# A reordering on TensorE in the heavy attention stage: select, scatter, turn two units, then project the queries

## The chip, the core and the metric

The kernel runs on one NeuronCore of a Trainium2 chip. The metric is the device time of one execution in microseconds (us), the median of several runs. The core's engines are named as in the profile: PE (TensorE, matrix products; its weight loads are the rows of PEld), DVE (VectorE), ACT (ScalarE), POOL (GpSimd) and SP (SyncE, which issues DMAs). Each engine runs its own instructions in program order; they wait for each other through semaphores.

## The reference

Four transformer layers over 16 sequences of 256 tokens with 128 channels (float32), each an attention and a feed-forward part with a residual and a layer norm. The change lies in the feed-forward part of the third layer (`L2_ffn`), in its heavy branch. The setup draws this part's `x` for another batch, but what runs is the 16 x 256 tokens of the stream.

```python
def route(x, routing_token, num_tokens):            # queries: 128 tokens, keys/values: 256
    s = einsum('bnd,d->bn', x, routing_token)
    scores = coor_descent(s, min(num_tokens * 9/8, n))
    sel_scores, sel_idx = top_k(scores, num_tokens)
...
light_out = light_local_attn(x, ...)                 # windows of 128 tokens
routed_q  = take_along_axis(x, idx_q[..., None], 1)  # the 128 chosen tokens of each sequence
routed_out = heavy_attn(routed_q, routed_kv, scores_kv, ...)   # 8 heads of 64, 128 queries x 256 keys
heavy_out = zeros_like(x).at[arange(b)[:, None], idx_q].set(routed_out * scores_q)
return light_out + heavy_out
```

## The kernel before

`l2_ffn` runs a routing start, a light attention stage (tiles named `a5l_...`), a routing finish and the heavy attention stage (`a5h_...`). Both attention stages, and that of layer four, come from one function, `wide_stage`. The heavy one lasts from about 1872 to 2118 us of the profiled execution.

`wide_stage` works in **slots**. A heavy slot handles one sequence (one of 16): four "units" of 128 queries x 512 score columns (two heads each). `all_quads` writes slots 0 to 3 out (`i == 0`), then runs a hardware loop of three rounds with four slots each (slots 4 to 15), then five tail slots in which only older work is finished. I number the slots 0 to 15 in order of time. In slot *s*, PE does, in the order written in the function `slot` under `block.tensor`:

- `scores` (L2554): q times k of sequence *s* into banks 0 to 3. It waits until the projections of this sequence have been copied out (`step_out0`, `step_out1`) and the older contents of the banks are done.
- `values` (L2586): probabilities times v of sequence *s-2*.
- `scatter` (L3138, from slot 3 on): puts the 128 results of sequence *s-3* back to their tokens by a product with its one-hot matrix, into bank 3. It waits for DVE's last score copy of the slot (`masked`, unit 3), which frees bank 3.
- group 0 of the projection steps, for sequence *s+1*: step "g" (L3041 and L3043) turns the one-hot matrix and picks the chosen tokens, into bank 0; ACT copies the result to `picked` (L3058); step "q" (L3050) multiplies `picked` by the query weights, into bank 1, and so waits for that copy; ACT copies it to `q` (L3060).
- `turn` of units 0 and 1 of sequence *s-1* (L2567): transposes of the probabilities into banks 4 and 5.
- group 1, the two key steps (L2983), then `project` (L2601) for sequence *s-2*, then group 2, the two value steps (L2980), then `turn` of units 2 and 3.

`picked` is a ring of four tiles, so the tile that g of slot *s* fills is the one that the scatter of slot *s* reads: ACT's copy L3058 waits for `scattered` (line `act.wait_ge(S["scattered"], ...)` in `SelectedSteps.act`).

ACT has a fixed order too: copy of the values (L2827), `picked`, `q`, the exponentials of units 0 and 1 (L2813, whose scores DVE has copied at L2667), the copy of turned unit 0 (L2820), the two key copies (L2991), the exponentials of unit 2, the copy of `project`'s result (L3132), the exponentials of unit 3 and the copy of turned unit 2. DVE copies scores, adds the scattered rows into X (L3146), copies turned units 1 and 3 (L2675), builds the one-hot matrix (L3032) and copies the values of group 2 (L3007). POOL normalizes (L2907) and copies x for later sequences.

Of the kernel before, what the change touches and what calls it, by code (L numbers as in the profile page):

```python
# [323 lines left out]
def total(i, each, k):  # L324

    return max(i * each + k, 0) if isinstance(i, int) else i * each + k
# [2046 lines left out]
NQ = 128  # L2373
# [41 lines left out]
def wide_stage(core, ctx, n, hd, steps, epilogue, moments=True, next_weights=(), ghost=None, weights_of=None, beside=None):  # L2415
# [3 lines left out]
    NQ, NE = len(hd.quads), len(hd.ends)  # L2419
# [14 lines left out]
    with mem:  # L2434
# [31 lines left out]
        groups = []  # L2466
# [20 lines left out]
        def in_loop(i):  # L2487
            return not (isinstance(i, int) and i == ROUNDS)

        def lagging(i, s, lag):  # L2490

            q = s - lag
            if (q >= 0 and in_loop(i)) or (q < 0 and not (isinstance(i, int) and i == 0)):
                return [q]
            return []

        def ending(i, s, lag):

            return [e for e in range(-E, E) if end_of(e) == s - lag and lagging(i, s, lag)]
# [6 lines left out]
        def halves_of(q):  # L2506


            b, k = divmod(q, NQ)
            return [(b * NH + before[k] + m, units, b * NE + e, place)  # L2510
                    for m, (units, e, place) in enumerate(hd.parts[k])]
# [27 lines left out]
        def _(pe):  # L2539
            pe.wait_ge(core.weights_in[wk], loaded_count(wk))  # L2540

            def scores(i, s):
                b, q = divmod(s, NQ)
                pe.wait_ge(S["masked"], total(i, 4 * R, 4 * s) + CREDIT)
                for lane in range(2):
                    pe.wait_ge(S[f"step_out{lane}"], total(i, NB * NS // 2, issued(s, lane)) + CREDIT)
                epilogue.wait_banks(pe, S, lambda lag: total(i, E, begun(s, lag)))
                for p in (0, 2):
                    pair = hd.quads[q][p:p + 2]
                    for m in range(len(pair[0][3])):  # L2550
                        for j, (qt, k0, kw, heads) in enumerate(pair, p):
                            c, odd = divmod(heads[m], 2)
                            r0 = 64 * odd
                            mm = pe.matmul(sbank[j][:, m * kw:(m + 1) * kw],  # L2554
                                           B["q"][b % 2][r0:r0 + 64, c, qt * P:(qt + 1) * P],
                                           B["k"][b % 2][r0:r0 + 64, c, k0:k0 + kw], start=True, stop=True)
                            if m == len(heads) - 1:
                                mm.then_inc(S["scores"], 1)

            def turn(i, q, j):  # L2560
                pe.wait_ge(S["normalized"], total(i, 4 * R, 4 * q + j + 1) + CREDIT)
                if j < 2:
                    pe.wait_ge(S[f"turned_out{j + 2}"], total(i, R, q) + CREDIT)
                else:
                    pe.wait_ge(S[f"turned_out{j - 2}"], total(i, R, q + 1) + CREDIT)
                for c in range(4):
                    mm = pe.transpose(tbank[j % 2][:, c * P:(c + 1) * P], pr[j][:, c * P:(c + 1) * P], ident)  # L2567
                mm.then_inc(S["turned"], 1)

            def values(i, s):  # L2570
                b, q = divmod(s % R, NQ)
                for g, units, e, place in halves_of(s):
                    for j in units:
                        pe.wait_ge(S[f"turned_out{j}"], total(i, R, s + 1) + CREDIT)
                    pe.wait_ge(S["evacuated"], total(i, NB * NH, g - 1) + CREDIT)
                    for p in units[::2]:
                        pair = hd.quads[q][p:p + 2]
                        qt, k0, kw, _ = pair[0]
                        nb = kw // P
                        for m in range(len(pair[0][3])):  # L2580
                            for kb in range(nb):
                                for j, unit in enumerate(pair, p):
                                    h = unit[3][m]
                                    r0, c0 = 64 * (h % 2), h // 2 % 4 * P
                                    col = (m * nb + kb) * P
                                    mm = pe.matmul(obank[g % 2][r0:r0 + 64, c0:c0 + P],  # L2586
                                                   B["v"][b % hd.ring][:, k0 // P + kb, h * 64:(h + 1) * 64],
                                                   pt[j][:, col:col + P], start=(kb == 0), stop=(kb == nb - 1))
                    mm.then_inc(S["values"], 1)
# [4 lines left out]
            def project(i, s, e):  # L2594
                y = epilogue.bank_of(e)
                masks_done(i, s, y)
                epilogue.wait_last(pe, S, lambda k: total(i, E, e + k))
                pe.wait_ge(S["evacuated"], total(i, NB * NH, halves_until(end_of(e)) + max(
                    m + 1 for m, (_, at, _) in enumerate(hd.parts[hd.ends[e % NE]]) if at == e % NE)) + CREDIT)
                for k in range(hd.chunks):  # L2600
                    mm = pe.matmul(sbank[y][:, 0:DM], on[e % 2][:, k * P:(k + 1) * P], epilogue.wo[:, k * DM:(k + 1) * DM],  # L2601
                                   start=(k == 0), stop=(k == hd.chunks - 1))
                mm.then_inc(S["projected"], 1)

            def scatter(i, s, e):
                masks_done(i, s, 3)
                epilogue.scatter(pe, B, S, i, e, sbank[3])

            def step(i, b, j, first=False):

                seq = NB * i + b
                if not first:
                    pe.wait_ge(S[steps.out_of(j)], steps.nth_out(seq, j) - 1 + CREDIT)
                    masks_done(i, b * NQ - NQ + j * NQ // NS, j % 2)
                elif j >= len(FIRST):
                    pe.wait_ge(S[steps.out_of(j)], steps.nth_out(0, j - len(FIRST)) + CREDIT)
                if j == 0:
                    pe.wait_ge(S["x_copied"], seq + 1 + CREDIT)
                steps.pe(pe, core, B, S, FIRST[j % len(FIRST)] if first else sbank[j % 2], j, b, seq).then_inc(S["step_mm"], 1)
# [1 line left out]
            for j in range(NS):  # L2621
                step(0, 0, j, True)

            def steps_in(i, s, group):
                if in_loop(i):
                    for j in groups[s % NQ][group]:
                        step(i, s // NQ + 1, j)

            def slot(i, s):
                if in_loop(i):  # L2630
                    scores(i, s)
                for q in lagging(i, s, LV):
                    values(i, q)
                if epilogue.scatters:
                    for e in ending(i, s, LS):
                        scatter(i, s, e)
                steps_in(i, s, 0)
                for q in lagging(i, s, LT):
                    turn(i, q, 0)
                    turn(i, q, 1)  # L2640
                steps_in(i, s, 1)
                for e in ending(i, s, LP):
                    project(i, s, e)
                steps_in(i, s, 2)
                for q in lagging(i, s, LT):
                    turn(i, q, 2)
                    turn(i, q, 3)

            all_quads(pe, slot)

        @block.vector
# [947 lines left out]
```

## Time and profile before

| what | us |
|---|---|
| median of 3 runs | 2816.76 (2816.34 to 2819.14) |
| the profiled execution | 2823.93 |
| its span | 2822.2 |
| slots 0 to 15 of the heavy stage, first scores to the last turned unit | 1882.1 to 2106.2 |
| a usual heavy slot, scores to scores | 14.0 to 14.4 |
| slot 4, the first of the hardware loop | 19.0 |

Over the whole span PE is busy 83% (with weight loads beside it, 65%), DVE 67%, ACT 49%, POOL 49%. TensorE's granted clock is a mean of 0.942 of full speed. "Busy" of PE includes the drain of pipelined products, so the starts of consecutive groups say more than their durations: what PE takes for a group is the distance from its start to the next group's start where nothing is waited for.

### The profile page before, as it was taken

The page shows a single profiled execution, that of the slowest core. Times are in us where ns is not written, and L with a number is a line of the kernel's source. Part 1 is how long each engine was busy: PE and PEld are TensorE (multiplying, and loading weights), DVE is VectorE, ACT ScalarE, POOL GpSimd, SP SyncE. Part 2 cuts the span into 40 slices and gives each one's busy share as a digit, 9 for nine tenths or more (in the row PEclk, how much of TensorE's full clock was granted, in tenths as well). Part 3 has the DMA queues.
Part 4 walks back from the last instruction along what each step waited for, and adds up shares of the span by engine and source line. Part 5 has one row for each costly group of instructions (what it writes and reads, how often), then busy time and mean ns, then how long its engine had stood idle before and what let it go on. Part 6 is the DMA issues. An engine that isn't in the chain of part 4 may idle for free. (4 is left out here: it accounts for less than half of the span.)

```text
span 2822.2 us, 72090 instructions
## 1 busy us (share of the span) xinstructions
PE 2353.0 (83%) x21404; PEld 1825.2 (65%) x21404; DVE 1897.4 (67%) x8141; ACT 1390.2 (49%) x3317; POOL 1385.6 (49%) x1580
## 2 busy tenths in 40 slices
PE   6888888778689980869999799958987999999986
PEld 5666666545366660857777577747775777777755
DVE  4666666656488872657888589955555777767746
ACT  2333333322366650646666456634554666666624
POOL 4666666400366644547778265623332554554501
PEclk9999999989799995989999899989998999999978
DMA  2000000033100011220000100000000000000001
GB/s 73 2 1 0 0 0 0 20 86 79 53 2 0 0 38 42 65 82 2 0 0 0 39 2 1 0 1 2 0 0 23 2 1 0 0 0 0 0 1 31
DMA packets 38281, 45.51 MB, mean 16 GB/s; under 512 B 6160, under 2 KB 28777, under 8 KB 37804
## 3 DMA queue, kind: packets, MB, share of 16 engines
q1 hardware_dynamic: 35820, 38.89, 4.9%
q0 software_dynamic: 2304, 4.79, 0.5%
q8 instruction: 67, 1.10, 0.2%
q14 instruction: 90, 0.74, 0.1%
HBM read 36.62 MB, written 9.74 MB: 16 GB/s over the span
## 5 line engine op out<-in xcount | busy, mean ns | idle before, releaser
L1102 POOL TENSOR_TENSOR a_sm<-a_sm,a_top 128x512 f32<-128x512 f32 x512 | 524.2, 1041 | 279.9 <-DVE a_top L900 278.0
L1025 ACT ACTIVATE a_pr<-a_sm 128x512 f32<-128x512 f32 x512 | 315.2, 626 | 239.8 <-POOL a_sm L1102 151.6
L900 DVE CUSTOM_DVE_ANT_0 a_sm<-bank,cst 128x256 f32<-128x256 f32 (+1 forms) x1024 | 301.0, 353 | 106.3 <-PE bank L762 104.2
L776 PE MATMUL bank<-cst,a_pr 128*128 128x128 f32 x2304 | 309.5, 276 | 1.3 <-ACT a_pt L1035 0.9
L2907 POOL TENSOR_TENSOR a_pr<-a_sm,a_rden 128x512 f32<-128x512 f32 x192 | 197.4, 1049 | 228.1 <-DVE a_rden L2693 227.7
L776 PEld LDWEIGHTS bank<-cst,a_pr 128*128 128x128 f32 x2304 | 257.0, 141 | 33.5 <-issue 23.6
L908 DVE COPY a_pt<-bank 128x512 f32<-128x512 f32 x272 | 186.7, 686 | 132.5 <-PE bank L776 132.4
L1035 ACT ACTIVATE a_pt<-bank 128x512 f32<-128x512 f32 x304 | 177.3, 589 | 87.9 <-PE bank L776 83.9
L2667 DVE CUSTOM_DVE_ANT_0 a_sm<-bank,cst 128x256 f32<-128x256 f32 (+1 forms) x512 | 149.9, 354 | 52.4 <-PE bank L2554 45.1
L796 PEld LDWEIGHTS bank<-a_pt,a_v 128*32 128x32 f32 x4608 | 119.6, 110 | 99.9 <-issue 89.1
L796 PE MATMUL bank<-a_pt,a_v 128*32 128x128 f32 x4608 | 156.5, 276 | 17.8 <-issue 6.9
L900 DVE CUSTOM_DVE_ANT_0 a_sm<-bank,a_bias 128x256 f32<-128x256 f32 (+1 forms) x512 | 148.4, 353 | 25.3 <-PE bank L762 21.9
L2983 PE MATMUL bank<-a_xs,W 128*128 128x256 f32 x544 | 142.0, 396 | 17.0 <-ACT a_q L2996 10.8
L762 PE MATMUL bank<-a_kx,a_q 32*128 32x512 f32 (+1 forms) x896 | 111.0, 576 | 41.2 <-DVE a_on L918 32.3
L2907 POOL TENSOR_TENSOR a5h_pr<-a5h_sm,a5h_rden 128x512 f32<-128x512 f32 x64 | 65.7, 1047 | 159.6 <-DVE a5h_rden L2693 159.6
L900 DVE DVE_READ_ACCUMULATOR2_ANT a_top<- 128x1 f32 x1536 | 127.9, 83 | 0.0
L2813 ACT ACTIVATE a_sm<-a_sm,a_top 128x256 f32<-128x256 f32 x256 | 127.1, 505 | 0.0
L1092 POOL COPY a_xs<-XT 128x256 f32 (+1 forms) x54 | 21.5, 400 | 209.3 <-SPq L629 209.3
L2983 PEld LDWEIGHTS bank<-a_xs,W 128*128 128x128 f32 x544 | 96.9, 194 | 41.3 <-ACT a_q L2996 17.6
L2554 PE MATMUL bank<-a_k,a_q 64*128 64x256 f32 (+1 forms) x1024 | 98.6, 337 | 17.8 <-ACT a_k L2996 9.4
L1040 ACT ACTIVATE a_osb<-bank 128x256 f32<-128x256 f32 (+1 forms) x96 | 43.8, 457 | 139.9 <-PE bank L796 139.9
L2827 ACT ACTIVATE a_on<-bank 128x512 f32<-128x512 f32 x64 | 38.3, 598 | 147.4 <-PE bank L2586 147.4
(493 smaller groups left out, 5982.8 us busy)
## 6 DMA issues: line engine op xcount, KB each, us to landing
f_spread<-gate_rows SPq DMA_DIRECT2D x16, 512.0 KB, 7.0
W<-in_l_w SPq DMA_DIRECT2D x2, 2048.0 KB, 9.9
x_sorted<-in_l_blank SPq DMA_DIRECT2D x4, 660.0 KB, 7.4
f_xin<-x_sorted SPq DMA_DIRECT2D x10, 264.0 KB, 2.8
X<-in_x SPq DMA_DIRECT2D x4, 512.0 KB, 7.7
a_bias<-bias_rows SPq DMA_DIRECT2D x1, 2048.0 KB, 7.5
X<-y_rows SPq DMA_DIRECT2D x8, 256.0 KB, 5.3
out_x<-X SPq DMA_DIRECT2D x8, 256.0 KB, 2.3
```

The costliest lines, as they stand in the source:

```text
L762: mm = pe.matmul(sbank[j][:, col:col + m * kw], B["q"][b][r0:r0 + rows, c, qt * P:(qt + 1) * P], B["kx"][b][r0:r0 + rows, x:x + m, 0:kw], ...
L776: mm = pe.transpose(tbank[j % 2][:, c * P:(c + 1) * P], pr[j][:, c * P:(c + 1) * P], ident)
L796: mm = pe.matmul(O[32 * group:32 * group + 32, blk * P:(blk + 1) * P], B["v"][b][:, kb, hd.slot[h], :], pt[j][:, col:col + P], start=(kb = ...
L900: ins = dve.tensor_tensor_reduce(sm[j][:, m * kw:(m + 1) * kw], sbank[j][:, m * kw:(m + 1) * kw], mk, 1.0, 3.0e38, ALU.add, ALU.min, top[: ...
L908: dve.tensor_copy(pt[j][:, :], tbank[j % 2][:, :]).then_inc(S[f"turned_out{j}"], 1)
L1025: act.activation(pr[j][:, :], sm[j][:, :], ACT.Exp, scale=-1.0).then_inc(S["probs"], 1)
L1035: act.activation(pt[j][:, :], tbank[j % 2][:, :], ACT.Copy).then_inc(S[f"turned_out{j}"], 1)
L1102: pool.tensor_tensor(whole, whole, top[:, qt, a:a + m].unsqueeze(2).to_broadcast([P, m, kw]), ALU.subtract).then_inc(S["shifted"], 1)
L2667: ins = dve.tensor_tensor_reduce(sm[s % 2 * 4 + j][:, m * kw:(m + 1) * kw], sbank[j][:, m * kw:(m + 1) * kw], mk, 1.0, 3.0e38, ALU.add, AL ...
L2813: ins = act.activation(part, part, ACT.Exp, bias=top[:, s % 2, j, m:m + 1], scale=-1.0, accum_out=den[:, s % 2, j, m:m + 1])
L2907: pool.tensor_tensor(pr[j][:, :].rearrange("p (h k) -> p h k", k=kw), sm[q % 2 * 4 + j][:, :].rearrange("p (h k) -> p h k", k=kw), rden[:, ...
L2983: mm = pe.matmul(bank[:, c * SEQ:(c + 1) * SEQ], w[:, a:a + P], xs[:, :], start=True, stop=True)
```

## The change

In a stage whose epilogue scatters (the heavy one alone), PE's group 0 is taken apart. Step g comes first, then the scatter, then the two turns, then step q. The new `part` argument cuts the group's list of steps; `first` holds one step in the heavy stage, and all of them in the other stages, where the order stays as it was. No other engine's program changes.

```diff
-            def steps_in(i, s, group):
+            def steps_in(i, s, group, part=slice(None)):
                 if in_loop(i):
-                    for j in groups[s % NQ][group]:
+                    for j in groups[s % NQ][group][part]:
                         step(i, s // NQ + 1, j)
 
             def slot(i, s):
@@
                 for q in lagging(i, s, LV):
                     values(i, q)
+                first = slice(0, 1 if epilogue.scatters else None)
+                steps_in(i, s, 0, first)
                 if epilogue.scatters:
                     for e in ending(i, s, LS):
                         scatter(i, s, e)
-                steps_in(i, s, 0)
                 for q in lagging(i, s, LT):
                     turn(i, q, 0)
                     turn(i, q, 1)
+                if epilogue.scatters:
+                    steps_in(i, s, 0, slice(1, None))
                 steps_in(i, s, 1)
```

One product of float32 is two rows in the profile's counts and one here (a transpose one in both). PE in one slot of the hardware loop, before, from values to the key steps (`a5h_ysb` is the projected result that is scattered, `a5h_pr` the normalized probabilities, `cst` the identity):

```order
L2586 MATMUL bank<-a5h_pt,a5h_v 64x128 x16
L2592 REGISTER_ALU
L3138 MATMUL bank<-a5h_ysb,a5h_picked 128x128 x2
L2613 ISA
L2592 REGISTER_ALU
L2618 REGISTER_ALU
L3041 MATMUL bank<-cst,a5h_onehot 128x128 x2
L3043 MATMUL bank<-a5h_onehot,a5h_xtok 128x128 x2
L2592 REGISTER_ALU
L3047 REGISTER_ALU
L3050 MATMUL bank<-a5h_picked,W 128x128 x4
L2567 MATMUL bank<-cst,a5h_pr 128x128 x8
```

PE at the same place of the changed kernel, where L3041, L3043, L3138, L3047 and L3050 have become L3044, L3046, L3141, L3050 and L3053:

```order
L2586 MATMUL bank<-a5h_pt,a5h_v 64x128 x16
L2613 ISA
L2592 REGISTER_ALU
L2618 REGISTER_ALU
L3044 MATMUL bank<-cst,a5h_onehot 128x128 x2
L3046 MATMUL bank<-a5h_onehot,a5h_xtok 128x128 x2
L2592 REGISTER_ALU
L3141 MATMUL bank<-a5h_ysb,a5h_picked 128x128 x2
L2567 MATMUL bank<-cst,a5h_pr 128x128 x8
L2592 REGISTER_ALU
L3050 REGISTER_ALU
L3053 MATMUL bank<-a5h_picked,W 128x128 x4
```

The scatter has moved behind g, and the eight transposes of the two turns (four each) stand between it and q.

PE in slot 2 of the changed kernel, written out ahead of the loop, where there is nothing to scatter yet; the value and key steps' lines have moved by three as well:

```order
L2586 MATMUL bank<-a5h_pt,a5h_v 64x128 x16
L3044 MATMUL bank<-cst,a5h_onehot 128x128 x2
L3046 MATMUL bank<-a5h_onehot,a5h_xtok 128x128 x2
L2567 MATMUL bank<-cst,a5h_pr 128x128 x8
L3053 MATMUL bank<-a5h_picked,W 128x128 x4
L2986 MATMUL bank<-a5h_xs,W 128x256 x4
```

Here only the turns have moved, from behind q to ahead of it.

## Rows read from the trace of the kernel before

**Rows 1.** Timeline, PE, slot 9: start us, us, engine line operation [idle before <-releaser]
```profile
2007.66 2.00 PE L2554 MATMUL bank<-a5h_k,a5h_q 64*128 64x256 f32 x16
2009.59 1.97 PE L2586 MATMUL bank<-a5h_pt,a5h_v 128*64 128x128 f32 x32
2012.01 0.71 PE L3138 MATMUL bank<-a5h_ysb,a5h_picked 128*128 128x128 f32 x4 [0.45 <-DVE a5h_top L2667]
2012.56 0.38 PE L3041 MATMUL bank<-cst,a5h_onehot 128*128 128x128 f32 x2
...
2013.96 1.16 PE L3050 MATMUL bank<-a5h_picked,W 128*128 128x128 f32 x8 [0.58 <-ACT a5h_picked L3058]
2014.96 1.04 PE L2567 MATMUL bank<-cst,a5h_pr 128*128 128x128 f32 x8
2015.83 1.89 PE L2983 MATMUL bank<-a5h_xs,W 128*128 128x256 f32 x8
...
2018.73 1.98 PE L2980 MATMUL bank<-W,a5h_xs 128*128 128x512 f32 x4
...
2021.70 2.00 PE L2554 MATMUL bank<-a5h_k,a5h_q 64*128 64x256 f32 x16
```

**Rows 2.** Timeline, ACT and then DVE, slot 9
```profile
2013.42 0.49 ACT L3058 ACTIVATE a5h_picked<-bank 128x384 f32<-128x384 f32 x1 [1.22 <-PE bank L3043]
...
2018.10 1.07 ACT L2991 ACTIVATE a5h_k<-bank 128x512 f32<-128x512 f32 x2
```
```profile
2019.98 1.61 DVE L3007 TENSOR_SCALAR a5h_v<-bank,VS 128x512 f32<-128x512 f32 x2 [0.74 <-PE bank L2980]
```

**Rows 3.** Timeline, PE, values and query step of slots 8 and 11
```profile
1995.42 1.97 PE L2586 MATMUL bank<-a5h_pt,a5h_v 128*64 128x128 f32 x32
...
1999.91 1.16 PE L3050 MATMUL bank<-a5h_picked,W 128*128 128x128 f32 x8 [0.66 <-ACT a5h_picked L3058]
...
2037.71 1.97 PE L2586 MATMUL bank<-a5h_pt,a5h_v 128*64 128x128 f32 x32
...
2042.02 1.16 PE L3050 MATMUL bank<-a5h_picked,W 128*128 128x128 f32 x8 [0.58 <-ACT a5h_picked L3058]
```

**Rows 4.** Timeline, PE, slot 2, where nothing is scattered
```profile
1906.45 1.97 PE L2586 MATMUL bank<-a5h_pt,a5h_v 128*64 128x128 f32 x32
1908.35 0.44 PE L3041 MATMUL bank<-cst,a5h_onehot 128*128 128x128 f32 x2
1908.63 0.61 PE L3043 MATMUL bank<-a5h_onehot,a5h_xtok 128*128 128x128 f32 x4
1909.91 1.13 PE L3050 MATMUL bank<-a5h_picked,W 128*128 128x128 f32 x8 [0.67 <-ACT a5h_picked L3058]
```

**Rows 5.** Timeline, PE, slot 6, scatter and query step
```profile
1969.58 0.71 PE L3138 MATMUL bank<-a5h_ysb,a5h_picked 128*128 128x128 f32 x4 [0.76 <-DVE a5h_top L2667]
...
1971.54 1.16 PE L3050 MATMUL bank<-a5h_picked,W 128*128 128x128 f32 x8 [0.58 <-ACT a5h_picked L3058]
```

**Rows 6.** Timeline, PE and one of ACT, slot 4
```profile
1938.50 0.71 PE L3138 MATMUL bank<-a5h_ysb,a5h_picked 128*128 128x128 f32 x4 [2.75 <-DVE a5h_top L2667]
...
1940.53 2.08 PE L3050 MATMUL bank<-a5h_picked,W 128*128 128x128 f32 x8 [0.66 <-ACT a5h_picked L3058]
...
1942.64 0.60 ACT L3060 ACTIVATE a5h_q<-bank 128x512 f32<-128x512 f32 x1 [2.17 <-PE bank L3050]
...
1944.11 3.17 PE L2983 MATMUL bank<-a5h_xs,W 128*128 128x256 f32 x8
...
1948.00 1.88 PE L2980 MATMUL bank<-W,a5h_xs 128*128 128x512 f32 x4
```

**Rows 7.** Stretches, slot 4: from:to, length, busy us (xcount) of each engine, PEclk, DMA
```profile
1940.00:1940.50 0.50, 0.00 (x0) 0.00 (x0) 0.17 (x2) 0.48 (x1) 0.00 (x0) 0.50 0.00 0
...
1946.50:1947.00 0.50, 0.50 (x3) 0.39 (x3) 0.25 (x1) 0.15 (x1) 0.50 (x2) 0.82 0.00 0
```

**Rows 8.** Waits in slot 9: engine line waited for, us in total, times, longest
```profile
PEld bank L2586 <- issue: 0.3, 1, 0.3
```

## The prediction

> **What bounds the kernel now.** Only the heavy stage changes, so I first look for what sets the length of one of its slots. I read the timeline of one slot of PE, then ACT's and DVE's rows of the same slot. In slot 9 PE stands still twice ahead of the query step: 0.45 us before the scatter, for DVE's copy of the last scores, and 0.58 us before q, for ACT's copy of `picked` [rows 1]. From q on, PE does not set the pace: q starts at 2013.96; ACT copies its product out, does the exponentials of two units and a turned copy, and starts its key copies at 2018.10 [rows 2]. The two copies take 1.07 us together with some overlap, so the first ends about 0.58 us after it began, at 2018.68. PE starts the value steps at 2018.73 [rows 1], because they need the bank that this copy frees. The distance q to value steps is 4.77 us. DVE copies the values out at 2019.98 after waiting for PE, until 2021.59 [rows 2], and the next scores start at 2021.70. So the chain of a slot is: scores, values, scatter, g, `picked`, q, ACT's queue up to the first key copy, value steps, DVE's copy, scores. **Moving q moves the slot's end one to one; moving PE's other work moves nothing.** A reader should check both halves of that in the rows.
>
> **The change, part by part.** I measure from the start of values (V) to the start of q (Q).
>
> *Before.* In eleven slots (3, 5 and 7 to 15) Q - V lies between 4.31 us (slot 11: 2042.02 - 2037.71) and 4.49 us (slot 8: 1999.91 - 1995.42) [rows 3]; the mean of the eleven is 4.39. Slots 4 and 6 stand apart (below).
>
> *After.* Step g follows values at once, since its bank was read by DVE long before; slot 2, which has nothing to scatter, shows values to g as 1908.35 - 1906.45 = 1.90 us [rows 4]. g's first two passes take 0.28 us there [rows 4]. A pass of 128 columns costs 0.109 us (eight in the turns: 2015.83 - 2014.96 = 0.87) [rows 1], so g's other four take 0.44 and g 0.72; all six at 0.109 would be 0.65. I take 0.69. Then the scatter: it would start at V + 2.59 plus a seam, while before it was released by DVE at V + 2.42 in slot 9 [rows 1]. DVE's last copy is therefore done just as g ends: that stall is covered by g. Scatter to next group is 2012.56 - 2012.01 = 0.55, of which 0.44 are products and 0.11 a seam between groups [rows 1]. The two turns take 0.87 [rows 1]. The seam between g and the scatter I can't see; other seams are 0 (turns to keys) to 0.13 (0.12 behind q: 2014.96 - 2013.96 is 1.00 for eight passes of 0.109) [rows 1], so I take 0.07. Sum: 1.90 + 0.69 + 0.07 + 0.55 + 0.87 = **4.08**, with bounds 4.02 and 4.15 from the seam and a little of g.
>
> *Is `picked` ready by then?* Its copy now waits for the scatter, since both use one tile of the ring of four. ACT takes a finished product 0.03 us after its end (q of slot 4: 1940.53 + 2.08, taken at 1942.64) [rows 6]; I allow 0.12. The copy takes 0.49, and in slot 9 q started 0.05 after its end (2013.91 to 2013.96) [rows 1, 2]. From the scatter's start, `picked` is there after 0.71 + 0.03 to 0.12 + 0.49 + 0.05 = 1.28 to 1.37 us, and PE has done scatter and turns after 0.55 + 0.87 = 1.42. The turns cover the copy, with a margin of 0.05 to 0.14 us.
>
> *Gain in the eleven slots:* 4.39 - 4.08 = 0.31 us each (0.24 to 0.37), **3.4 us** (2.6 to 4.1). It is much less than the two stalls together (about 1.03 us) because the turns, 0.87, have moved on to the chain; they were off it.
>
> *Slot 6:* DVE was later here and the scatter waited 0.76 [rows 5]. Scatter to q was 1.96, and becomes 1.42: **0.5 us**.
>
> *Slots 1 and 2:* no scatter, so g to q is 1.56 now [rows 4] and becomes 0.70 + 0.07 + 0.87 = 1.64, up to 1.70: a loss of **0.1 each**. Slot 0 has no turns and stays.
>
> *Slot 4* is the dear one. PE waits 2.75 us for DVE, then 0.66 more before q, and q and what follows runs at double length (q 2.08 us against 1.16) [rows 1, 6]: the granted clock is 0.50, the lower level of 1.2 GHz, at 1940.0, and is back at 2.4 GHz within 1946.5 to 1947.0 [rows 7]. Q to value steps is 1948.00 - 1940.53 = 7.47 us instead of 4.77. DVE's delay stays. After the change q can start at 1938.50 + 1.42 = 1939.92. If the clock falls at the same moment, ACT gets q's result near 1942.03 instead of 1942.64 [rows 6]; keys then start near 1941.9, last 3.0 at this clock (3.17 with the drain) [rows 6], `project`, eight passes, takes 1.75 instead of 0.87, and the value steps start at 1946.7 instead of 1948.00: **1.3 us**. If the clock held, it would be 1939.92 + 4.77 = 1944.7: 3.3 us. If it cost nothing in either kernel: 0.6. I take 1.3, as the stall that came before the fall is still there.
>
> *Everything else.* Key steps and `project` start over 1.1 us earlier and then PE waits before the value steps, some 1.1 us in one piece; it costs nothing. The second key step needs the bank that ACT's q copy frees, 0.60 after it starts; that is about Q + 1.85, just when the first key step ends, so no stall of more than 0.05, and none on the chain. DVE's scattered addition moves 0.2 us back; the row after it on DVE is far from late. Its copy of turned unit 1 can come 2 us earlier. POOL's order and inputs stay.
>
> **Sum:** 3.4 + 0.5 - 0.2 + 1.3 = **5.0 us**. Against the profiled execution: span 2822.2 to 2817.2, and 2823.93 to 2818.9. The median of the runs is 7.2 us below the profiled execution; I carry the same difference over: 2816.76 - 5.0 = **2811.8**. A measurement here can tell about 0.2% (5.6 us) from no change, so my forecast is within it, by little.
>
> **Rivals.**
>
> *A. The clock does not fall in slot 4.* For it: g now runs inside the 2.75 us stall and the 0.66 us behind it are gone, so PE's idle time around the fall drops from 3.4 to about 2.1 us. Against: 2.1 us of idle in one piece remain. Slot 4 gives 3.3 instead of 1.3: gain 7.0, time 2809.8, faster. Chance 0.27.
>
> *B. The clock falls once more.* PE's idle time in a slot is now in one piece ahead of the value steps. Against it: the work is the same and the slot is shorter, so the idle time of a slot in all gets less. One fall costs what slot 4 lost, 7.47 - 4.77 = 2.7: gain 2.3, time 2814.5. Chance 0.13.
>
> *C. The seams close.* Values are 32 products that run in pairs, so 16 x 0.109 = 1.75. If all groups follow without a seam, V to Q is 1.75 + 0.65 + 0.44 + 0.87 = 3.71, and then `picked` decides: scatter at V + 2.40 (just when DVE is done in slot 9), + 1.37 = 3.77. Gain 0.62 in eleven slots, 6.8; with 0.5 and 1.3 of slots 6 and 4 it is 8.6: time 2808.2, faster. Against: 1.90 and 0.55 are measured where nothing is waited for [rows 1, 4]. Chance 0.04. (The Trainium skill, "TensorE: Matmul & The Clock Gate", Part 2 on what happens when a matmul is issued, says that PE pulls the next weight load ahead of running matmuls; by that rule the seams would vanish. The trace agrees at turns to keys and disagrees at scatter to g, 0.11 us.)
>
> *D. The seams are wider: slower.* Three seams that stood behind a stall until now (values to g, g to scatter, turns to q) may show the instructions that compute wait values. PE's weight loads stand 0.3 us in "issue" ahead of values [rows 8]. With 0.33 for each: 1.75 + 0.33 + 0.69 + 0.33 + 0.55 + 0.87 + 0.33 = 4.85, 0.46 later than before in eleven slots (+5.1), +0.7 each in slots 1 and 2, +0.2 in slot 6, -0.9 in slot 4 (scatter to q 1.75 against 2.03, and 0.6 of what the clock took): 2816.8 + 5.8 = 2822.6, slower. The gain is gone from seams of 0.22 each (0.66 instead of the 0.22 in my sum, 0.44 x 11 = 4.8). Against: values themselves started 1.93 us after the scores, behind that same weight load [rows 1], some 0.2 us of seam at most. Chance 0.05.
>
> *E. `picked` comes too late.* If `picked` comes 0.3 us later than 1.37 after the scatter (ACT now passes a second semaphore, fed by PE), the turns don't cover it and Q moves by 0.25: gain 0.06 in eleven slots (0.7), 0.25 in slot 6, -0.2, 1.0 in slot 4: 1.8 in all, 2815.0. This is the case in which the query step still waits for its input, so that the change hardly does what it says. Chance 0.11.
>
> **How the numbers follow.** My forecast, with 4.0 to 6.0 around it (2810.8 to 2812.8), has 0.40. Range: from 2808.5 to 2816.8; the low end covers A and nearly C, the high end B, E and a run of no gain; about 0.83 inside. Faster by over 0.2%: most of A (0.23), C (0.04), and the part of my own case above 5.6 us (0.11): 0.38. Slower: D and a little for more falls of the clock: 0.07. Within 0.2%: 0.55.
>
> **What the changed profile would show.** Right: no stall before g; at most 0.1 us before the scatter in most slots; q right behind the turns at V + 4.1; q to value steps still 4.77; some 1.1 us of PE idle before the value steps, released by ACT's key copy; slots of 13.7 to 13.9 us. Wrong, if: a stall before q on `picked` (E); seams over 0.15 (D); value steps released by something else than ACT's key copy, or q to value steps longer than 4.77. Slot 4 decides between 1.3 and 3.3 us: look at the granted clock from 1940 to 1947.

## The result and the profile after

The changed kernel takes 2812.42 us (median of 10 runs, 2808.24 to 2813.41) against 2816.61 us for the kernel before (10 runs, 2815.09 to 2820.09). The two medians are 4.2 us apart; the ratio on record, which comes from all the runs and is not the quotient of the medians, is 0.998 with a 95% interval of 0.9971 to 0.9988, which is 5.6 us less (3.4 to 8.2). The forecast was 2811.8. The time came out close, but not all of the working did: the stage itself gained nearly twice what I had summed up, and part of that is not in the medians.

Slot 9 of the changed kernel, PE's timeline, the counterpart of [rows 1] (start us, us, engine line operation, idle before and its releaser; line numbers above 2640 are three higher than before, and some more in the last experiments):

```profile
2001.23 2.00 PE L2554 MATMUL bank<-a5h_k,a5h_q 64*128 64x256 f32 x16
2003.16 1.97 PE L2586 MATMUL bank<-a5h_pt,a5h_v 128*64 128x128 f32 x32
2005.06 0.44 PE L3044 MATMUL bank<-cst,a5h_onehot 128*128 128x128 f32 x2
2005.33 0.61 PE L3046 MATMUL bank<-a5h_onehot,a5h_xtok 128*128 128x128 f32 x4
2005.78 0.61 PE L3141 MATMUL bank<-a5h_ysb,a5h_picked 128*128 128x128 f32 x4
2006.23 1.04 PE L2567 MATMUL bank<-cst,a5h_pr 128*128 128x128 f32 x8
2007.10 1.09 PE L3053 MATMUL bank<-a5h_picked,W 128*128 128x128 f32 x8
2008.03 1.98 PE L2986 MATMUL bank<-a5h_xs,W 128*128 128x256 f32 x8
2009.84 1.05 PE L2601 MATMUL bank<-W,a5h_on 128*128 128x128 f32 x8
2011.80 1.98 PE L2983 MATMUL bank<-W,a5h_xs 128*128 128x512 f32 x4 [0.90 <-ACT a5h_k L2994]
...
2014.76 2.00 PE L2554 MATMUL bank<-a5h_k,a5h_q 64*128 64x256 f32 x16
```

Both stalls ahead of the query step are gone, and one of 0.90 us has appeared before the value steps, released by ACT's key copy. ACT and DVE in the same slot, the counterpart of [rows 2]:

```profile
2006.49 0.49 ACT L3061 ACTIVATE a5h_picked<-bank 128x384 f32<-128x384 f32 x1 [0.71 <-PE bank L3141]
2008.23 0.60 ACT L3063 ACTIVATE a5h_q<-bank 128x512 f32<-128x512 f32 x1 [1.25 <-PE bank L3053]
...
2011.16 1.06 ACT L2994 ACTIVATE a5h_k<-bank 128x512 f32<-128x512 f32 x2
```
```profile
2011.04 1.27 DVE L3035 TENSOR_SCALAR a5h_onehot<-W,rank 128x128 f32<-128x128 f32 x2
2013.05 1.61 DVE L3010 TENSOR_SCALAR a5h_v<-bank,VS 128x512 f32<-128x512 f32 x2 [0.74 <-PE bank L2983]
```

The copy of `picked` is released by the scatter (L3141), not by g, as the ring of four demands, and it ends at 2006.98, 0.12 us before q starts at 2007.10. Slot 9 has fallen from 14.04 us [rows 1] to 2014.76 - 2001.23 = 13.53 us.

Slot 4, the counterpart of [rows 6] and [rows 7]; the last two rows are stretches (from:to, length, busy time of PE, PEld, DVE, ACT and POOL, granted clock, DMA):

```profile
1937.60 0.71 PE L3141 MATMUL bank<-a5h_ysb,a5h_picked 128*128 128x128 f32 x4 [1.09 <-DVE a5h_top L2670]
1938.15 1.04 PE L2567 MATMUL bank<-cst,a5h_pr 128*128 128x128 f32 x8
1939.02 1.06 PE L3053 MATMUL bank<-a5h_picked,W 128*128 128x128 f32 x8
...
1943.69 1.98 PE L2983 MATMUL bank<-W,a5h_xs 128*128 128x512 f32 x4 [0.90 <-ACT a5h_k L2994]
```
```profile
1937.00:1941.00 4.00, 3.40 (x25) 3.12 (x26) 1.87 (x8) 1.37 (x3) 1.41 (x2) 1.00 0.00 0
1941.00:1945.00 4.00, 3.10 (x15) 2.17 (x15) 1.48 (x4) 4.00 (x16) 1.96 (x2) 1.00 0.00 0
```

The clock stayed at 1.00 (2.4 GHz), and q to value steps is 4.67 us here instead of 7.47. Scores to scores, slot 4 fell from 19.04 to 15.57 us.

The readings below use four lengths taken from each profile's PE timeline: the start of the stage's first scores (**ahead**); first scores to the start of the last scatter, less slot 4 (**slots**); **slot 4** alone; and the rest of the span (**behind**). "Slots" turned out to repeat within 0.06 us between executions of one kernel, while the medians move by some us, so it is the finest instrument here.

| kernel | slot 9 | slots | slot 4 | ahead | behind | median us | ratio (95%) |
|---|---|---|---|---|---|---|---|
| before | 14.04 | 216.75 | 19.04 | 1882.1 | 704.3 | 2816.61 | |
| changed | 13.53 | 210.38 | 15.57 | 1881.9 | 703.7 | 2812.42 | 0.9980 (0.9971-0.9988) |
| e3, before again | 14.04 | 216.75 | 17.36 | 1880.4 | 699.5 | 2815.13 | 0.9993 (0.9984-1.0002) |
| e4, changed again | 13.53 | 210.38 | 15.54 | 1877.4 | 703.8 | 2810.49 | 0.9980 (0.9971-0.9989) |
| e10, changed, third | 13.53 | 210.37 | 15.53 | 1880.8 | 704.1 | 2812.24 | 0.9981 (0.9972-0.9990) |
| e12, changed, fourth | 13.53 | 210.40 | 15.69 | 1881.1 | 703.8 | 2808.70 | 0.9973 (0.9961-0.9985) |
| e1, turns only | 14.06 | 217.00 | 17.73 | 1878.7 | 702.5 | 2816.56 | 0.9996 (0.9987-1.0005) |
| e2, g first only | 13.53 | 210.34 | 16.84 | 1877.6 | 702.9 | 2807.77 | 0.9963 (0.9950-0.9976) |
| e9, g first, again | 13.53 | 210.36 | 16.77 | 1883.9 | 699.8 | 2805.73 | 0.9960 (0.9946-0.9973) |
| e11, g first, third | 13.54 | 210.40 | 16.89 | 1879.2 | 696.3 | 2805.72 | 0.9962 (0.9950-0.9974) |
| e5, changed + ACT keys early | 13.05 | 203.65 | 16.68 | 1882.9 | 702.8 | 2806.50 | 0.9962 (0.9947-0.9977) |
| e6, before + ACT keys early | 13.66 | 211.39 | 15.79 | 1874.3 | 699.4 | 2802.79 | 0.9957 (0.9941-0.9973) |
| e7, g first + ACT keys early | 13.15 | 204.98 | 15.08 | 1879.7 | 703.1 | 2803.27 | 0.9951 (0.9936-0.9965) |
| e8, changed + keys earlier, one-hot early | 12.38 | 193.83 | 14.53 | 1880.1 | 701.9 | 2793.91 | 0.9918 (0.9904-0.9931) |

Each ratio of an experiment is to runs of the kernel before made beside it on the same chip; the medians of those were 2815.82 (e1 to e4), 2816.70 (e5 to e7), 2818.85 (e8 to e10) and 2816.37 (e11, e12). Apart from the first two rows, the column "median us" should therefore be compared only within such a set.

### The profile page after: what moved, and what is told of

Read it like the earlier page. It is cut to its first block and busy times, and to the rows that moved or that the text cites. A ratio compares the mean times of both kernels' runs of the same rounds, so it can differ in the third digit from the quotient of the medians.

```text
span 2811.5 us, 72090 instructions
## 1 busy us (share of the span) xinstructions
PE 2346.5 (83%) x21404; PEld 1820.4 (65%) x21404; DVE 1896.4 (67%) x8141; ACT 1388.9 (49%) x3317; POOL 1383.5 (49%) x1580
## 5 line engine op out<-in xcount | busy, mean ns | idle before, releaser
L2986 PE MATMUL bank<-a_xs,W 128*128 128x256 f32 x544 | 141.8, 396 | 16.8 <-ACT a_q L2999 10.7
```

The source lines that it names most:

```text
L2986: mm = pe.matmul(bank[:, c * SEQ:(c + 1) * SEQ], w[:, a:a + P], xs[:, :], start=True, stop=True)
```

## Which half of the change does it

The change has two halves: g goes ahead of the scatter, and the turns go ahead of q. Each was tried alone. First the turns alone, with the scatter back in front:

```diff
                 first = slice(0, 1 if epilogue.scatters else None)
-                steps_in(i, s, 0, first)
                 if epilogue.scatters:
                     for e in ending(i, s, LS):
                         scatter(i, s, e)
+                steps_in(i, s, 0, first)
```

> Undoes the move of the scatter: PE does scatter, g, turns, q. My theory: only the start of the query step (Q) counts. The scatter again waits for DVE until about V + 2.42 (V: start of values), then scatter 0.55, g 0.69, turns 0.87: Q at V + 4.45 to 4.5 against 4.39 in the kernel before and 3.94 in the changed one. From q to the value steps 4.70 us, as in the changed kernel, against 4.77. Slot 14.0 to 14.1 us, time within 1.5 us of the kernel before, and 0.1 us lost in each of slots 1 and 2. Rival (each PE stall that is filled is won): the 0.58 us stall before q is gone in 13 slots, 7 us faster than the kernel before. Clock in slot 4: may fall as before, since the scatter still waits 2.75 us there.

Measured: Q - V 4.51 us, slots 217.00 us, 0.25 us *more* than before; ratio 0.9996. The loss of 0.1 us in each of slots 1 and 2 did not come (11.45 and 13.10 us, as before). Slot 9, PE:

```profile
2004.92 1.97 PE L2586 MATMUL bank<-a5h_pt,a5h_v 128*64 128x128 f32 x32
2007.34 0.71 PE L3141 MATMUL bank<-a5h_ysb,a5h_picked 128*128 128x128 f32 x4 [0.45 <-DVE a5h_top L2670]
2007.89 0.38 PE L3044 MATMUL bank<-cst,a5h_onehot 128*128 128x128 f32 x2
...
2009.43 1.06 PE L3053 MATMUL bank<-a5h_picked,W 128*128 128x128 f32 x8
...
2014.09 1.98 PE L2983 MATMUL bank<-W,a5h_xs 128*128 128x512 f32 x4 [0.90 <-ACT a5h_k L2994]
```

The stall before q is filled in every slot and nothing is won: PE waits 0.90 us before the value steps instead. The rival, that each filled stall of PE is won, falls. The stall before q was 0.58 us, the turns put in its place 0.87.

Then g ahead of the scatter alone, with the turns back behind q:

```diff
+                if epilogue.scatters:
+                    steps_in(i, s, 0, slice(1, None))
                 for q in lagging(i, s, LT):
                     turn(i, q, 0)
                     turn(i, q, 1)
-                if epilogue.scatters:
-                    steps_in(i, s, 0, slice(1, None))
```

> Undoes the move of the turns: PE does g, scatter, q, turns. My theory: picked is ready 1.25 us after the scatter's start (0.71 to its end and ACT, 0.49 copy, 0.05), so Q = V + 1.90 + 0.72 + 1.25 = V + 3.87, and q to value steps is 4.77 as where q starts after a stall; Q + 4.77 = V + 8.64, the same as in the changed kernel (3.94 + 4.70 = 8.64). The slot is 13.5 us as there, slots 1 and 2 lose nothing, so the time is within 1 us of the changed kernel, about 6 us faster than the kernel before. Rival (the turns between are what wins): q waits about 0.6 us for picked, so the slot is 0.4 to 0.6 us longer than in the changed kernel, 5 to 8 us in all, close to the kernel before.

> PE order g, scatter, q, turns once more. Its first run had the same slots as the changed kernel to 0.04 us in all (slot 4 apart), but its times stood 3 to 4 us below it. Theory: that was the scatter of the rest of the program, and this time the difference to the changed kernel in the same call is within 2 us. Rival: the turns' place costs something outside the slots, and the difference is 3 to 4 us again.

> PE order g, scatter, q, turns a third time, beside the changed kernel on one chip. Twice its median stood below the changed kernel's (by 2.7 and 6.5 us) although the slots in its profiles are the same and its slot 4 is 1.2 us longer. If the place of the turns costs 3 to 6 us somewhere outside the slots seen, the median is 3 to 6 us below again and the profile shows where (time ahead of the first scores of the stage, or behind its last scatter). If it was scatter, the two are within 2 us of each other.

Measured: slots of 210.34, 210.36 and 210.40 us, those of the changed kernel (210.37 to 210.40) to 0.06 us. Slot 9 of e2, PE:

```profile
2000.18 1.97 PE L2586 MATMUL bank<-a5h_pt,a5h_v 128*64 128x128 f32 x32
2002.08 0.44 PE L3044 MATMUL bank<-cst,a5h_onehot 128*128 128x128 f32 x2
...
2002.80 0.61 PE L3141 MATMUL bank<-a5h_ysb,a5h_picked 128*128 128x128 f32 x4
2004.05 1.16 PE L3053 MATMUL bank<-a5h_picked,W 128*128 128x128 f32 x8 [0.64 <-ACT a5h_picked L3061]
...
2008.81 1.98 PE L2983 MATMUL bank<-W,a5h_xs 128*128 128x512 f32 x4
```

q starts at V + 3.87, 0.07 us earlier than with the turns ahead of it, although PE waits 0.64 us for it. From q to the value steps it is 4.76 us in e2, and 4.70 in the changed kernel, where q comes behind the turns: ACT takes the product 1.19 us after q's start in e2 and 1.13 in the changed kernel, and the rest is equal. So in the slots **the whole gain is g's move**, and the turns' move is worth nothing.

The medians say more. The g-first kernel stood 2.7, 6.5 and 3.0 us below the changed kernel in the three sets of runs that had both, though its slot 4 is 1.2 us longer. I had expected "within 1 us" for e2 and "within 2 us" for e9, and the third set missed 2 us as well. It is the same sign three times, though the single times of the two kernels overlap in every set. The profiles of e2 and e9 don't show this difference: these two executions took 2809.55 and 2812.53 us, those of the changed kernel beside them (e4, e10) 2808.89 and 2812.57. Only the third pair differs, 2804.67 (e11) against 2812.79 (e12), and there 7.5 us of the 8 lie behind the stage (696.3 against 703.8 us), in code that is the same in both. The part behind the stage was the shorter in e2 and e9 too (702.9 and 699.8, against 703.8 and 704.1), but slot 4, and in e9 the part ahead of the stage, took that back.

The stretches of e11 and of e12, from 0 to 10, 30 to 50 and 600 to 640 us behind the last scatter's start, show the granted clock (third number from the end):

```profile
2106.49:2116.49 10.00, 4.06 (x18) 2.94 (x19) 6.74 (x29) 2.89 (x5) 0.00 (x0) 0.73 0.07 15
2136.49:2156.49 20.00, 13.72 (x93) 10.31 (x92) 11.52 (x61) 11.84 (x32) 9.92 (x10) 1.00 0.00 0
2706.49:2746.49 40.00, 40.00 (x152) 25.40 (x152) 17.99 (x106) 7.00 (x14) 0.00 (x0) 0.85 0.00 1
```
```profile
2107.23:2117.23 10.00, 4.06 (x18) 2.94 (x19) 6.74 (x29) 2.88 (x5) 0.00 (x0) 0.62 0.13 17
2137.23:2157.23 20.00, 15.46 (x87) 11.05 (x85) 11.61 (x60) 8.86 (x22) 7.95 (x8) 0.83 0.00 0
2707.23:2747.23 40.00, 40.00 (x124) 23.59 (x123) 15.39 (x83) 4.13 (x9) 0.00 (x0) 0.70 0.00 1
```

In the changed kernel's run the clock is lower in all three, and PE gets through fewer products in 40 us (124 against 152). But e11 is the extreme: over the 20 us of the middle row the other thirteen profiles all show 0.83. Over the 40 us of the last row the clock is 0.70 or 0.71 in the four profiles of the changed kernel and in the first of the kernel before, 0.71 to 0.74 in e1, e2, e5, e7 and e8, 0.80 in e3, e6 and e9 and 0.85 in e11. The time behind the stage goes with it: 703.7 to 704.3, 701.9 to 703.1, 699.4 to 699.8 and 696.3 us. Over the first 10 us it is 0.62 to 0.64 in the first five of these, and 0.66 to 0.75 in the others.

All the runs together, most of them without a profile, agree. The median of their mean granted clocks is 0.9475, 0.947 and 0.9485 for g first (e2, e9, e11) and 0.946, 0.944 and 0.946 for the changed kernel beside them (e4, e10, e12). Within e12 alone, executions at 0.943 and 0.944 took 2812.8 and 2812.7 us, and those at 0.947 to 0.949 took 2806.3 to 2806.5. So the difference of the medians goes with the granted clock, and as in the profiles it is g first whose clock falls in slot 4, it must get more of it outside the slots. What sets that clock is open. The place of the turns alone does not: e5 has PE's order of the changed kernel and 0.74 over the first 10 us. One profile is one execution, and nothing I ran varies the moment at which the stage ends while leaving all else alone. That the turns' place costs something behind the stage is a correlation.

## How much of it is the clock in slot 4

> The kernel before once more, for its spread and for the clock in slot 4. If the 3.5 us that slot 4 gave in the two profiles is the clock's, and the clock falls there in some executions only, this profile may show slot 4 at 16 to 17 us and a span some 2.7 us shorter than 2822.2. If the fall is bound to the order of the work, slot 4 is 19.0 us again.

> The changed kernel once more. Theory that the order of the work decides: slot 4 takes 15.6 us with the clock at full, as in its first profile. Rival that it is chance: in some profile slot 4 takes some 18 us at 1.2 GHz and the span is 2 to 3 us longer. The other slots are 13.5 us in either case.

> The changed kernel a third time, beside the one above. Slots 13.53 us again; slot 4 15.6 us if its clock holds in this order always, 16.7 to 18 if it fell by chance only in the others. Ratio to the kernel before 0.9975 to 0.998.

> The changed kernel a fourth time, on the chip of the run above. Slots 13.53 us, slot 4 15.5 us if the clock holds in this order again. Ahead of the first scores 1877 to 1882 us and behind the last scatter 703 to 704 us, as in its other profiles.

The kernel before: 19.04 and 17.36 us, the clock falling in both but for a shorter time in e3. I had 16 to 17 us if the fall is a matter of chance, and a span some 2.7 us shorter; it was 8.2 us shorter, of which 1.7 are in slot 4. The PE timeline of e3 shows q slow (2.08) and the key steps already at full pace (1.89, against 3.17 in [rows 6]):

```profile
1938.59 2.08 PE L3050 MATMUL bank<-a5h_picked,W 128*128 128x128 f32 x8 [0.66 <-ACT a5h_picked L3058]
1940.46 1.69 PE L2567 MATMUL bank<-cst,a5h_pr 128*128 128x128 f32 x8
1941.98 1.89 PE L2983 MATMUL bank<-a5h_xs,W 128*128 128x256 f32 x8
```

The changed kernel: 15.57, 15.54, 15.53 and 15.69, clock at full four times. e2, e9 and e11 fell (16.8 to 16.9), e1 too (17.73). So in the orders tried without other edits the clock held only in the one that has neither a wait for `picked` behind the scatter nor a scatter ahead of g. But e5, which has that same PE order, fell (16.68), while e6, which has the order before, and e7, which has g first's, held (15.79 and 15.08). So PE's order does not settle it alone; whether it shifts the odds, seven falls in fourteen profiles are too few to show. What the order alone gives in slot 4 can be had from e6: its usual slots are 0.38 us shorter than the kernel before's, so without a fall the kernel before would take about 15.79 + 0.38 = 16.2 there, 0.6 more than the changed kernel. That is an estimate. By it the clock's share of the 3.47 us between the two first profiles is 2.9, and of the 1.79 us between e3 and the changed kernel 1.2.

## Is ACT's queue what binds a slot

If the chain from q to the value steps is ACT's queue, taking something out of that queue must show in full, once PE's own work is out of the way. The copy of turned unit 0 stands ahead of the key copies and can go behind them. I did this on the changed kernel, on the kernel before and on g first:

```diff
                     probs(i, s, 1)
                 aside(i, s, 1)
+                if epilogue.scatters:
+                    steps_in(i, s, 1)
                 copies(i, s, (0, 1))
-                steps_in(i, s, 1)
+                if not epilogue.scatters:
+                    steps_in(i, s, 1)
```

> The changed kernel with one more move, on ACT in the heavy stage alone: the two key copies come ahead of the copy of turned unit 0. My theory: ACT's queue between q and the first key copy sets the slot. That copy takes 0.48 us of the queue, so q to value steps falls from 4.70 to 4.22 us, PE's wait before the value steps from 0.90 to 0.42, the slot from 13.5 to 13.05: about 7 us faster than the changed kernel, 11 to 13 us faster than the kernel before. Rival (DVE's one-hot matrix, which stands ahead of its value copies and ends 1.27 us after the reciprocal, takes over): value steps 0.48 earlier but the scores only 0.1 to 0.3 earlier, 2 to 4 us in all.

Measured: slot 9 13.05 us, slots 203.65, 6.7 us below the changed kernel. That is the theory's number (about 7), to 0.3 us; by the ratio the kernel is 10.7 us faster than the kernel before, where I had 11 to 13. The value steps come 10.08 us after the scores instead of 10.57, still released by ACT:

```profile
2005.83 1.09 PE L3056 MATMUL bank<-a5h_picked,W 128*128 128x128 f32 x8
...
2010.04 1.99 PE L2986 MATMUL bank<-W,a5h_xs 128*128 128x512 f32 x4 [0.42 <-ACT a5h_k L2997]
```

q to value steps is 4.21 us. DVE's one-hot matrix did not take over: DVE stood 0.26 us before the value copies and was released by PE.

> The kernel before with the same move on ACT (key copies ahead of the copy of turned unit 0). My theory: there PE's own work stands close behind ACT: turns 0.87, keys 1.73 and project 0.9 after q, so q to value steps can only fall from 4.77 to about 4.5. The slot gets 0.2 to 0.3 us shorter, 3 to 4 us in all. If the full 0.48 came (7 us), PE's work would have had more room than I think; if nothing came, the value steps were not bound by ACT.

Measured: slots 211.39, 5.4 us below the kernel before; I had 3 to 4. In slot 9 q to value steps is 4.49, as expected:

```profile
2000.21 1.16 PE L3053 MATMUL bank<-a5h_picked,W 128*128 128x128 f32 x8 [0.58 <-ACT a5h_picked L3061]
...
2003.81 1.05 PE L2601 MATMUL bank<-W,a5h_on 128*128 128x128 f32 x8
2004.70 1.88 PE L2983 MATMUL bank<-W,a5h_xs 128*128 128x512 f32 x4
...
2007.57 0.70 PE L2554 MATMUL bank<-a5h_k,a5h_q 64*128 64x256 f32 x4
```

What I had missed is that value steps that follow `project` without a wait take 1.88 us and not 1.98, so the scores came 2.87 us later instead of 2.97. Its median, 13.9 us below the kernel before (12.1 by the ratio, 7.6 to 16.6), is more than the 5.4 us of its slots and the 1.6 to 3.3 of slot 4: the profile was also 8 us early ahead of the stage, in code that no kernel here changes. e6 even has a lower median than e5, whose slots are 7.7 us shorter. With five runs each, the medians of these kernels don't rank them.

> PE order g, scatter, q, turns (the turns' move undone) with the key copies ahead on ACT. My theory: with the turns back between q and the keys, PE is the bound after q: 4.5 us instead of 4.22, so Q + 4.5 = V + 8.37 against V + 8.16 with the turns ahead of q. The slot is 0.2 us longer than with the changed kernel's order and the same ACT order, 2 to 3 us in all: here the move of the turns pays. Rival: no difference, the turns' move is worth nothing in any order.

Measured: slots 204.98, 1.3 us above e5. The theory had 2 to 3, with the right sign. With ACT's queue shortened, PE's work after q (turns, keys, `project`) is the bound, and the turns ahead of q save 0.10 us per slot, half of what I had worked out, again because the value steps start without a wait. So in the slots the turns' move is worth something only once ACT is faster. The whole kernel does not show it: the median of e7 is 3.2 us *below* that of e5, the ratios are within each other's intervals, and slot 4 took 15.08 us in e7 and 16.68 in e5.

A last kernel makes two moves on the changed kernel: the key copies go ahead of the exponentials of unit 1 as well, and DVE's one-hot matrix goes ahead of its reciprocal (its old place is left out in this stage).

```diff
                     probs(i, s, 0)
+                if epilogue.scatters:
+                    steps_in(i, s, 1)
+                if in_loop(i):
                     probs(i, s, 1)
...
+                if epilogue.scatters and in_loop(i):
+                    steps.prepare(dve, core, B, S, s + 2, NB * i + s + 2)
                 if in_loop(i):
                     recip(i, s, 0)
```

> The changed kernel with two more moves in the heavy stage: on ACT the two key copies come ahead of the exponentials of unit 1 (not only ahead of the turned copy), and on DVE the one-hot matrix is built ahead of the reciprocal instead of behind it. My theory: ACT now needs q copy, unit 0 and one key copy after q, so the first key copy ends near Q + 3.3 us and PE's own work (keys, project) is the bound: q to value steps 3.7 us. DVE has nothing long left ahead of its value copies, so scores follow 2.97 us after. Slot 12.6 us against 13.53 in the changed kernel and 13.05 with the keys ahead of the turned copy alone; the fifteen slots without slot 4 take about 198 us against 210.4 and 203.7. Time about 18 us below the kernel before. Rival (the delayed reciprocal takes over: POOL's normalizing or DVE's order holds the value copies): slot stays at 13.05 or grows.

Measured: slot 9 12.38 us, slots 193.83 (I had 12.6 and 198), median 2793.91, ratio 0.9918 (0.9904 to 0.9931), which is 23 us: the best version here, faster than both kernels. Of the 0.22 us that I missed in a slot, 0.06 lie between q and the value steps (3.64 us, I had 3.7) and 0.09 between these and the scores (2.88, I had 2.97). The two moves were not tried one by one. Slot 9, PE and DVE around the value steps:

```profile
1998.18 1.05 PE L2601 MATMUL bank<-W,a5h_on 128*128 128x128 f32 x8
...
1999.07 1.88 PE L2989 MATMUL bank<-W,a5h_xs 128*128 128x512 f32 x4
...
2000.11 0.18 DVE L2696 RECIPROCAL a5h_rden<-a5h_den 128x4 f32<-128x4 f32 x1 [3.39 <-ACT a5h_sm L2818]
2000.38 1.45 DVE L3016 TENSOR_SCALAR a5h_v<-bank,VS 128x512 f32<-128x512 f32 x2
```

PE's own work is now the bound up to the value steps, and DVE's value copies follow the reciprocal, which waits for ACT's exponentials of unit 1.

## Why the prediction was right where it was, and wrong where it wasn't

**The bound: right.** Moving q moved the slot's end, moving the turns alone did not, and in the usual slots the value steps waited for ACT's key copy in each kernel that left ACT's order alone. e1, e2 and e5 each show it from another side. In the kernel before, and in e2, this wait is so short that only the weight load of the value steps shows it (slot 9, before):

```profile
2018.73 0.30 PEld L2980 LDWEIGHTS bank<-W,a5h_xs 128*128 128x128 f32 x2 [0.30 <-ACT a5h_k L2991]
```

So "moving PE's other work moves nothing" holds only while ACT is behind PE, and there PE was close: e6, which takes 0.48 us out of ACT's queue, got 0.28 of it between q and the value steps, and then PE was the bound.

**V to q in the usual slots: the term was too small.** I had 4.39 - 4.08 = 0.31 us; it was 4.39 - 3.94 = 0.45. Values to g came out as taken (1.90) and the turns too (0.87); g took 0.72. The seams did not: g to scatter has none, and scatter to turns takes 2006.23 - 2005.78 = 0.45 and not 0.55. The step that failed is taking the 0.55 from a scatter that had just been released from a stall. PE's weight loads show what the 0.11 us are. The first load of the scatter of slot 9, before and after:

```profile
2012.01 0.52 PEld L3138 LDWEIGHTS bank<-a5h_ysb,a5h_picked 128*128 128x128 f32 x4 [0.69 <-DVE a5h_top L2667]
```
```profile
2005.67 0.53 PEld L3141 LDWEIGHTS bank<-a5h_ysb,a5h_picked 128*128 128x128 f32 x4
```

Before, the load starts with the products, at 2012.01 [rows 1]; after, it starts 0.11 us ahead of them, which start at 2005.78. Where it does not start ahead, the scatter takes 0.11 us more. That is so behind a wait (slot 4 of the changed kernel, 1938.15 - 1937.60 = 0.55, and e1), and also in the tail of the kernel before, where a scatter follows values directly:

```profile
2109.28 0.52 PEld L3138 LDWEIGHTS bank<-a5h_ysb,a5h_picked 128*128 128x128 f32 x4 [0.17 <-issue]
2109.29 0.71 PE L3138 MATMUL bank<-a5h_ysb,a5h_picked 128*128 128x128 f32 x4
2109.84 1.04 PE L2567 MATMUL bank<-cst,a5h_pr 128*128 128x128 f32 x8
```

My rival C had closed seams at a chance of 0.04, with the argument against it that 0.55 was measured where nothing is waited for; [rows 1] show the opposite, a wait of 0.45 us. Two of its seams were closed, though the 0.15 us behind values stayed, where the load of g does not start ahead either (both at 2005.06); g takes 0.72 us there, and 0.66 in e1, where it follows the scatter with its load ahead. (The rule of the Trainium skill named there, in "TensorE: Matmul & The Clock Gate", Part 2, that the next weight load is pulled ahead of running products, agrees with the scatter of the changed kernel, 0.11 us ahead; the first loads behind values, which start with their products, do not show it.) q's first load starts 0.07 us ahead of its products in the changed kernel and with them before, and so q to value steps fell from 4.77 to 4.70, which I had at unchanged. Together a usual slot gained 0.51 us (14.04 to 13.53), 0.20 more than forecast.

**Slots 1 and 2: 0.2 us of loss were forecast, none came** (11.44 and 13.10 us in both kernels): q started 0.04 later and its products took 0.04 less, 1.09 against 1.13.

**Slot 6: 0.5 forecast, 0.62 measured** (14.36 to 13.74).

**`picked` in time: right.** It was ready at scatter + 1.25 (e2), below the 1.28 I had as the least; PE needed 1.32, not 1.42, so the margin was 0.07 us. E falls.

**Slot 4: rival A happened in the profile.** I had 1.3 us for the clock falling again and 3.3 if it held; it held, and the slot gained 3.47. The idle time ahead of the scatter, which I had at 2.1 us in one piece, was in two: g too waited for DVE, 0.66 us, and then the scatter 1.09. These two pieces are not the reason by themselves, since e2 has both and its clock fell, with 0.58 us more ahead of q.

**The sum and the median.** In the two first profiles the stage gained 6.4 us in its slots and 3.5 in slot 4, 9.8 in all, where I had 5.0, and the span fell by 10.7. The median fell by 4.2. The step that failed here is to carry a gain seen in one profile over to the median as it is: the first profile of the kernel before was 7.3 us above its own median, with the longest fall of the clock in slot 4 that was seen and one of the lowest clocks behind the stage (0.64 over 10 us, 0.70 over 40), while that of the changed kernel was 1.0 above. Against the second profile of the kernel before (2814.0, e3), the first of the changed kernel (2811.5) stands only 2.5 us lower: 8.2 won in the stage, 4.2 lost behind it and 1.5 ahead of it. By ratio the gain is 5.6 us, and 5.6, 5.4 and 7.6 in the three repeats (e4, e10, e12). So the forecast's 5.0 was met by a larger gain in the stage and a part outside it that I had not foreseen; that the time came out in the middle of the forecast is partly luck.

**B and D fall.** The clock did not fall in any usual slot in spite of the 0.90 us pause, and no seam grew.

## What to carry to other kernels

Before filling an engine's stall, ask whether what fills it was on the chain: the scatter's stall was filled with g, which was on it, and that gave everything; q's stall was filled with turns, which were not, and that gave nothing by itself. When a filled stall reappears further down with another releaser (here ACT's key copy), the next edit belongs to that engine's queue: two such moves on ACT and DVE (e8) were worth 16.6 us more in the slots, against the 6.4 of the change. And take the price of a step from rows in which the engine comes to it as it will after the change: for PE, look whether the group's first weight load starts ahead of its products.

## What the runs showed of the hardware that I had not expected

- A slot's work repeats to hundredths of a microsecond between executions and chips (13.53 us), while the same code ahead of the stage took 1874.3 to 1883.9 us, and the same code behind it 696.3 to 704.3 us. Nearly all of the kernel's spread lies there and in slot 4, and behind the stage it goes with the granted clock (0.70 to 0.85 over the same 40 us).
- Where the first weight load of the scatter starts with its products, and not 0.11 us ahead of them, the next group comes 0.11 us later (0.55 against 0.45 us), behind a wait and directly behind values alike. Value steps take 1.98 us of busy time where their load waited for ACT, and 1.88 where it did not.
- A fall of the clock in slot 4 lasted differently in two profiles of one program (q at 2.08 us in both, the key steps at 3.17 and 1.89).
